# One more block product of a two-level Winograd product as seven 256x256 products (Q4, groups 2 to 4)

## The reference

```python
y   = einsum('bct,bcd->bdt', x, weights[condition])   # x: (64, 64, 1024), weights[condition]: (64, 64, 64)
xf  = y.reshape(4096, 1024)
G   = zeros(4096, 64); the 16 largest of xf @ Wr.T get softmax gates
h   = einsum('nd,krd->nkr', xf, A)                    # A: 64 x 16 x 1024, so h is 4096 x 1024
out = einsum('nkr,kdr->nd', h * G[:, :, None], B)     # again 1024 -> 1024
return x + 2.0 * out
```

## Time and profile before

| | us |
|---|---|
| median of 3 runs | 715.38 (714.88 to 715.78) |
| the profiled execution | 715.06 |
| its span | 713.3 |
| PE busy | 707.2 (99%) |
| DVE busy | 499.8 (70%) |
| ACT busy | 259.5 (36%) |
| DMA moved | 186.85 MB, 262 GB/s over the span |

### The profile page before, as it was taken

One profiled execution on the slowest core, in us unless ns is written; L12 is line 12 of the kernel. 1 busy time (PEld: TensorE's weight loads), 2 busy tenths in 40 slices (PEclk: granted clock), 3 DMA queues, 4 the chain that ended last, 5 costly groups with the idle time before them and its releaser, 6 DMA issues.

```text
span 713.3 us, 10128 instructions
## 1 busy us (share of the span) xinstructions
PE 707.2 (99%) x3522; PEld 599.8 (84%) x3522; DVE 499.8 (70%) x897; ACT 259.5 (36%) x475; POOL 1.6 (0%) x6
## 2 busy tenths in 40 slices
PE   9999999999999999999999999999999999999997
PEld 8888888888888888888898888888889888888886
DVE  5888999995558796745572868774557297777665
ACT  5675553525326431223332552132233353213210
POOL 0000000000000000000000000000000000000000
PEclk9999999999999999999999999999999999999999
DMA  9976679666798968467588775765758787536756
GB/s 323 405 299 279 219 278 397 221 245 228 272 371 329 335 239 296 154 231 242 201 305 344 282 280 165 263 202 193 284 204 317 304 307 256 194 129 201 253 209 221
DMA packets 59716, 186.85 MB, mean 262 GB/s; under 512 B 9874, under 2 KB 12562, under 8 KB 59154
## 3 DMA queue, kind: packets, MB, share of 16 engines
q1 hardware_dynamic: 57746, 182.68, 70.6%
q10 hardware_dynamic: 1920, 3.54, 1.4%
HBM read 136.38 MB, written 49.81 MB: 261 GB/s over the span
## 4 chain that ended last, share of the span: by engine, by line
PE 98%; DVE 1%; issue 1%; POOL 0%; DVEq 0%; POOLq 0%
PE Pb L572 42%; PE Pb L605 38%; PE Cb L554 8%; PE S L636 4%; PE Pb L625 4%; PE T L643 1%; PE T L690 0%; PE T L684 0%; PE Pb L588 0%; DVE Q L913 0%; PE Cb L650 0%; DVE Ox L913 0%; PE S L650 0%; PE T L650 0%; DVE Op L913 0%
## 5 line engine op out<-in xcount | busy, mean ns | idle before, releaser
L572 PE MATMUL Pb<-Op,Wt 128*128 128x512 f32 x984 | 237.6, 391 | 0.0
L605 PE MATMUL Pb<-Wt,Op 128*128 128x512 f32 x912 | 218.1, 391 | 0.0
L572 PEld LDWEIGHTS Pb<-Op,Wt 128*128 128x128 f32 x984 | 183.3, 188 | 37.5
L605 PEld LDWEIGHTS Pb<-Wt,Op 128*128 128x128 f32 x912 | 170.0, 188 | 34.9 <-DVE Op L913 0.4
L913 DVE TENSOR_TENSOR Q<-Pb,Q 128x1024 f32<-128x1024 f32 (+1 forms) x77 | 82.4, 1077 | 64.4 <-issue 54.3
L750 ACT COPY R<-Cb 128x512 f32<-128x512 f32 x60 | 35.1, 587 | 144.3 <-PE Cb L554 144.2
L913 DVE TENSOR_TENSOR Op<-R,Op 128x512 fp32r<-128x512 f32 x93 | 61.6, 684 | 22.7 <-ACT Op L724 22.7
L572 PE MATMUL Pb<-Ox,Wt 128*128 128x512 f32 x300 | 75.6, 390 | 0.0
L605 PE MATMUL Pb<-Wt,Ox 128*128 128x512 f32 x288 | 73.0, 391 | 0.0
L572 PEld LDWEIGHTS Pb<-Ox,Wt 128*128 128x128 f32 x300 | 56.1, 188 | 11.6
L913 DVE TENSOR_TENSOR Cq<-Pb,Cq 128x1024 f32<-128x1024 f32 (+1 forms) x40 | 40.2, 1006 | 32.2 <-issue 22.9
(11 more groups left out here) (94 smaller groups left out, 505.2 us busy)
## 6 DMA issues: line engine op xcount, KB each, us to landing
Wt<-Wd SPq DMA_DIRECT2D x177, 512.0 KB, 5.5
Wd<-Wt SPq DMA_DIRECT2D x56, 512.0 KB, 4.8
Q<-in_x SPq DMA_DIRECT2D x32, 512.0 KB, 5.6
xc<-in_x SPq DMA_DIRECT2D x24, 512.0 KB, 3.9
out<-Q SPq DMA_DIRECT2D x19, 512.0 KB, 4.0
out<-Q SPq DMA_DIRECT2D x26, 256.0 KB, 3.7
Wd<-xc SPq DMA_DIRECT2D x7, 512.0 KB, 6.3
BR<-in_B SPq DMA_DIRECT2D x3, 1024.0 KB, 8.1
```

The costliest lines, as they stand in the source:

```text
L572: t = e.matmul(Pb[:, j, :], Wt[:, k, a, 128 * c:128 * c + 128], part((USES1[m], s, c), z), start=fresh and (c, a, z) == (0, 0, 0), stop=(c ...
L605: t = e.matmul(Pb[:, i, :], part((USES2[m], s, c), a)[:, 128 * i:128 * i + 128], Wt[:, k, z, :], start=fresh and (c, a, z) == (0, 0, 0), s ...
```

## The change

Q4 (`m` = 4) joins Q3 as seven 256x256 products in groups 2 to 4 (`TWO`). Its operand G22 is split in seven forms, with four more sums on VectorE; the forms that are sums take Cq[:, 3] (Q4) and `u` (Q3) as their place. S4's sums move from Q7's steps to Q6's. Before the seven products Q7's accumulated banks are added to Q7's and to Q4's place. Of the four tiles that are added to the place of seven-product blocks, three are added ahead of these, the fourth behind the first of the seven.

The weights of Q4 need seven more forms. They are made in group 1's second stage, at the steps 20 to 26: ScalarE copies (`made_hi`, behind `unit_hi`, ahead of the step's operand splits), VectorE subtracts (`made_lo`, ahead of `unit_lo`) and makes four sums between, SyncE stores a form to `Wd` in the step after (`made_store`, behind `weights_load`, ahead of `unit_store` and `q_store`). They go through the two halves of one buffer, so that the copy of form n (n from 2) waits until the store of form n-2 has landed.

```diff
+TWO = [(), (4, 6), (4, 6), (4, 6)]
+LEVEL = (4, 6)
...
-MADE_AT = [0, 2, 4, 6, 12, 13, 15]
+MADE_AT = {4: [20, 21, 22, 23, 24, 25, 26], 6: [0, 2, 4, 6, 12, 13, 15]}
...
 def steps(s, m):
-    return 7 if s and m == 6 else 4
+    return 7 if m in TWO[s] else 4
...
+def cond_step(s, m, i):
+    step = 4 * m + i
+    if s + 1 == NS or i > 3:
+        return None
+    if s == 0:
+        return SPREAD.index(step) if step in SPREAD else None
+    return step // 3 if step in range(2, 24, 3) else None
...
 def splits_second(s, m, c):
+    if m == 3 and 4 in TWO[s]:
+        return [("G22", k) for k in ((0, 1), (2,), (3,), (4,))[c]]
+    if m == 4 and 4 in TWO[s]:
+        return [("G22", c + 5)] if c < 2 else [("S1", c - 2)] if c < 6 else []
...
# SyncE
+            def made_store(m, n):
+                e.wait_ge(v_made, made_before(m) + n + 1)
+                e.dma_start(Wd[UNITS + 7 * LEVEL.index(m) + MADE[n]], made(m, n)).then_inc(o_made[n % 2], 16)
...
                for m, name in enumerate(SECOND):
                    for i in range(steps(s, m)):
                        step = 4 * m + i
-                        weights_load(BASE[s] + 28 + 4 * m + (i if s and m == 6 else 0))
+                        weights_load(BASE[s] + USED[s].index(UNITS + 7 * LEVEL.index(m) + i if m in TWO[s] else 28 + 4 * m))
+                        if s == 0 and step - 1 in MADE_AT[4]:
+                            made_store(4, MADE_AT[4].index(step - 1))
                         if s == 0 and m < 6:
                             unit_store(32 + step)
...
# TensorE, two(s, m, k)
                 elif k == 3:
-                    e.wait_ge(v_out, out_done(s, 5, 3, 1))
+                    e.wait_ge(v_out, out_done(s, m - 1, 2, 1))
...
# ScalarE
+            def made_hi(m, n):
                 if n >= 2:
-                    e.wait_ge(o_form[n % 2], 16 * (n // 2))
+                    e.wait_ge(*stored(m, n - 2))
+                elif m == 6:
+                    e.wait_ge(p_cond, rows_number(1, 6 + n, 0))
                 else:
-                    e.wait_ge(p_cond, rows_number(1, 6 + n, 0))
+                    e.wait_ge(v_wlo, 52)
                 if n > 2:
-                    e.wait_ge(v_twow, n - 2)
-                e.copy(made(k, 0).bitcast(F32R), weight2(k)).then_inc(a_twohi, 1)
+                    e.wait_ge(v_wsum, 4 * LEVEL.index(m) + n - 2)
+                e.copy(made_part(m, n, 0).bitcast(F32R), weight2(m, MADE[n])).then_inc(a_made, 1)
...
                             unit_hi(32 + step)
+                        if s == 0 and step in MADE_AT[4]:
+                            made_hi(4, MADE_AT[4].index(step))
                         for name, c in splits_second(s, m, i):
...
# VectorE
+            def made_lo(m, n):
+                e.wait_ge(a_made, made_before(m) + n + 1)
+                add(made_part(m, n, 1).bitcast(F32R), weight2(m, MADE[n]), made_part(m, n, 0), v_made, ALU.subtract)
+                a11, a12, a21, a22 = weight2(m, 0), weight2(m, 1), weight2(m, 4), weight2(m, 6)
                 if n == 1:
+                    if m == 6:
+                        e.wait_ge(v_wlo, UNITS)
+                    add(a21, a11, a21, v_wsum, ALU.subtract)
                 elif n == 2:
...
+                    add(a22, a22, a21, v_wsum, ALU.subtract)
...
+                    add(a11, a22, a11, v_wsum)
+                elif n == 3:
+                    add(a12, a12, a22, v_wsum, ALU.subtract)
...
# VectorE, drain_second
                 add(to, P, to, v_out, n=2)
-                if s and name == "Q5":
-                    to = Q[:, 3 + i:5 + i, 512:1024]
-                    e.wait_ge(v_out, out_done(s, 2, i))
-                    add(to, P, to, v_out, n=2)
+                if m + 1 in TWO[s]:
+                    tile, half = INTO[SECOND[m + 1]][0] + i, INTO[SECOND[m + 1]][1]
...
+                    if i == 1:
+                        to = Q[:, tile - 1:tile + 1, 512 * half:512 * half + 512]
+                        add(to, P, to, v_out, n=2)
+                    else:
+                        to = Q[:, tile - 1, 512 * half:512 * half + 512]
+                        add(to, Pb[:, 2, :], to, v_out)
...
# VectorE, drain_two
+                add(to, Pb[:, BANK2[r], :].rearrange("p (i n) -> p i n", n=256), to, v_out)
+                if r == 0:
+                    tile, half = INTO[SECOND[m]]
+                    to = Q[:, tile + 3, 512 * half:512 * half + 512]
+                    add(to, Pb[:, 3, :], to, v_out)
...
# VectorE, the second stage
+                        if s == 0 and step in MADE_AT[4]:
+                            made_lo(4, MADE_AT[4].index(step))
                         if s == 0 and m < 6:
                             unit_lo(32 + step)
```

More of the change, by code:

```diff
@@ L22 @@
 SENT = -3.4028234663852886e38
+TWO = [(), (4, 6), (4, 6), (4, 6)]
+LEVEL = (4, 6)
+USED = [[*range(28)] + [n for m in range(7) for n in (
+    range(56 + 7 * LEVEL.index(m), 63 + 7 * LEVEL.index(m)) if m in TWO[s] else range(28 + 4 * m, 32 + 4 * m))]
+    for s in range(NS)]
+BASE = [sum(len(u) for u in USED[:s]) for s in range(NS + 1)]
 FIRST = ["P2", "P1", "P5", "P3", "P6", "P7", "P4"]
@@ L143, in chunk_done, with chunk_done2, form_done, level_before @@
     return 49 * s + 7 * m + 4 + c
+def chunk_done2(s, m, c):
+    return 7 * sum(k not in TWO[r] for r in range(s + 1) for k in range(7 if r < s else m)) + 4 + c
 def tile_done2(s, m, i):
[L148 to L157, removed]
-def split_done(name, s, c):
-    return 4 * s + c + 1 if name != "S4" or s == 0 else 7 * s - 3 + c + 1
+    return chunk_done2(s, m, 0) - 4 + (i + 1 if i < 3 else 7)
+def form_done(s, m, k):
+    return 7 * level_before(s, m) + k + 1
+def level_before(s, m):
+    return sum(len(TWO[r]) for r in range(s)) + TWO[s].index(m)
+def split_done(name, s, c):
+    m = USES2.index(name) if name in USES2 else 0
+    return sum(steps(r, m) for r in range(s)) + c + 1
+def outs():
+    order = []
+    for s in range(NS):
+        for m in range(7):
+            if m in TWO[s]:
+                order += [(s, m, 0, 0), (s, m - 1, 3, 1), *((s, m, i, 0) for i in range(1, 7))]
+            elif m + 1 in TWO[s]:
+                order += [(s, m, i, r) for i, r in ((0, 0), (1, 0), (0, 1), (1, 1), (2, 0), (3, 0), (2, 1))]
+            else:
+                order += [(s, m, i, 0) for i in range(4)]
+    return {key: n + 1 for n, key in enumerate(order)}
+OUTS = outs()
 def out_done(s, m, i, r=0):
[L168 to L171, removed]
+    return OUTS[s, m, i, r]
 def unit_use(n):
     s = max(s for s in range(NS) if BASE[s] <= n)
[L177 to L183, removed]
+    return s, USED[s][n - BASE[s]]
 def rows_number(s, i, a):
@@ L315, in quarter, with weight2, made, made_before @@
             return block[:, 2 * c:2 * c + 2, 256 * n:256 * n + 256]
-        def weight2(k):
+        def weight2(m, k):
             c, n = [(0, 0), (1, 0), (1, 1), (0, 0), (0, 1), (1, 0), (1, 1)][k]
[L320 to L329, removed]
+            return (u if m == 4 else raws[2])[:, 2 * c:2 * c + 2, 256 * n:256 * n + 256]
+        def made(m, n):
+            return raws[1][:, 2 * (n % 2):2 * (n % 2) + 2, :].rearrange("p a n -> p (a n)") if m == 4 else xc[:, n % 2, :]
+        def made_before(m):
+            return 7 * LEVEL.index(m)
+        def stored(m, n):
+            return o_made[n % 2], 16 * (n // 2 + 1) + (64, 48)[n % 2] * LEVEL.index(m)
+        def made_part(m, n, a):
+            return made(m, n)[:, 512 * a:512 * a + 512].rearrange("p (c n) -> p c n", n=256)
+        def out2(m, r):
+            (tile, half), (t, n) = INTO[SECOND[m]], INTO2[r]
+            at = 512 * half + 256 * t
+            return Q[:, tile + 2 * n:tile + 2 * n + 2, at:at + 256]
+        def places2(m):
+            return (Cq[:, 1, :, :], Cq[:, 3, :, :]) if m == 4 else (Cq[:, 2, :, :], u[:, :, :])
         def source(name, s, c):
@@ L444, in x_load @@
                     if s == 2:
-                        e.wait_ge(o_form[i], (64, 48)[i])
+                        e.wait_ge(*stored(6, 6 - i))
                 else:
@@ L486, in _ @@
                         weights_load(BASE[s] + step)
[L487 to L490, removed]
+                        if s == 1 and step - 1 in MADE_AT[6]:
+                            made_store(6, MADE_AT[6].index(step - 1))
                         if s == 0 and 6 <= step < 10:
@@ L700, in _ @@
                         step = 4 * m + i
-                        if s and m == 6:
-                            two(s, i)
+                        if m in TWO[s]:
+                            two(s, m, i)
                         else:
                             second(s, m, i)
-                        if more and step in (SPREAD if s == 0 else range(2, 24, 3)):
-                            k = SPREAD.index(step) if s == 0 else step // 3
+                        k = cond_step(s, m, i)
+                        if k is not None:
                             e.wait_ge(l_w[k], 32 * (s + 1))
@@ L935, in made_lo @@
```

(1 more changed line is left out.)

185 lines of the change are left out of this document (98 added, 87 removed).

## The result

The changed kernel takes 736.47 us (median of 4 runs, 736.13 to 737.77) against 715.45 before: 1.0298 times as long, 95% interval 1.0280 to 1.0316. The profiled execution took 736.34 us, its span is 734.6, so the span grew by 21.3 us. The prediction said 734, range 728 to 741.

A forecast was written before the change was run, and what follows sets the result against it. TensorE, busy 99%, was taken to bound the kernel. From 715.06 us, less 1.8 gained, plus 18.5 for waits and 2.1 for the clock, came 733.9; with 0.3 for the median 734.2, said as 734, range 728 to 741.

The forecast's parts named there:

- The ring: End of group 1: drain, store, landing, copy, subtraction, drain in series, three times round; TensorE 18.5 us late.
- store 0: First form's store in group 1, behind an output store: issued at 182.15, landed after 5.5 us at 187.65.
- S4's fourth part: Split read by tile 24 of group 1: ready at 193.9, wanted at 188.14, so 5.9 us late.
- Store 3: Form store near the end of group 1: issued at 200.75, 5.64 us after the drain's end at 195.1.
- Store 3's landing: Queued behind four weight loads: 7.0 us, landing at 207.75, with copy 5 and y21 part two behind it.
- store 4's: Landing with the queue nearly empty: 3.8 us, at 215.1, ahead of copy 6 and y21 parts three and four.
- the stores are hidden: Rival for group 1: stores issued when forms are ready cost nothing; 713.6 us, 0.4 us of slack; 5% faster, 2% no change.
- The clock: TensorE's restart after standing still for 6 and 7 us: 2.1 us lost once, between 0 and 4.2.
- The gain: Seven narrow products for Q4 in groups 2 to 4: 0.83 + 0.83 + 0.15 = 1.8 us gained.
- What is late next is that load: Group 4's last block: the sixth product waits for its last two weights' load, so adding the fourth tile later gains 0.

The follow-up runs named there:

- outputs_later: Changed kernel, with the eight output stores of Q5 and Q3 in group 1 issued behind the group's last step: 721.32 us, 1.0087 of the kernel before.
- pool_queue: Changed kernel, with the stores of Q4's seven weight forms issued from GpSimd's queue instead of SyncE's: 722.86 us, 1.0111 of the kernel before.
- pair_drain: Changed kernel, but Q4's forms made in group 2, Q3's last two form loads earlier, fourth tile added with the third before the seven products: 720.03 us, 1.0065.
- shift: Kernel before, with only S4's sums moved to Q6's steps and the fourth tile added behind the first product, no forms of Q4: 715.35 us, 1.0002.
- shift_early: As shift, with the loads of Q3's last two weight forms issued ahead of the output store: 714.47 us, 0.9988 of the kernel before.
- before_early: Kernel before, with only the loads of Q3's last two weight forms issued early: 715.02 us, 0.9995 of the kernel before.
- spread: Changed kernel, with fourteen forms of Q3 and Q4 spread over group 2's first stage and Q3's last two form loads early: 714.42 us, 0.9986.

## Why the prediction was right

The mechanism, its place and its size came out.

**The ring.** Predicted 18.5 us, measured 20.4. Its members are the chain above. By steps: store 0 predicted at 182.15, issued at 182.45, landed after 5.65 us (5.5). S4's fourth part predicted ready at 193.9, TensorE went on at 194.98. Store 3 predicted at 200.75, issued at 202.54: I had let store 1's landing (6.31 us, from 185.44) hide behind ScalarE's other copies, and it ended 1 us later than they did; the rest is SyncE's list, which took 6.5 us from the drain's end to store 3 instead of 5.64. Store 3's landing took 8.3 us against 7.0, store 4's 3.0 against 3.8. These are the mis-sized terms: 1.8 + 1.3 - 0.8, less the 0.34 us by which the whole kernel starts later, 1.9 us in all. That the last of the three erred the other way is luck; it brought the sum 0.8 us nearer. One wait was left out: group 2's first tile also waits for the drain of its bank, 7.6 us (213.99); it ends ahead of the wait for y21's third part, so it costs nothing. outputs_later and pool_queue show the lock of stores and drains to be worth 13 to 15 us. In outputs_later a wait of 5.0 us for landings in series through two buffers is left, with 1.8 us for the clock behind it.

My rival "the stores are hidden" (5%) was worked out with every store issued as its form is ready: store 3 near 186 and landed by 193. No run met that condition. In outputs_later store 3 was issued at 190.50, 3.9 us after its form was ready, and in pool_queue at 190.63, 4.3 us after; the times were 721 and 723, not 713.6. The rival's working also took 7.2 us at most for a landing, where 9.1 and 9.4 were measured behind the four loads. With its slack of 0.4 us either alone could undo it; whether it would hold with stores issued at once stays open.

**The clock.** Predicted one loss of 2.1 us, measured 1.91 at group 2's first tiles. The size came out, but the place is another than I had in mind. In the standstill of 7.6 us the granted clock fell from 1.00 to 0.50, the lower level of 1.2 GHz. TensorE had stopped at 206.4 and the clock was 1.00 until 210; at the end of the kernel before it had fallen within 2 us of the last matmul. It was 0.50 from 214 to 216, for most of the six matmuls; what that costs is hidden, since TensorE waits 2.4 us behind them for y21's third part. At 218 the clock was back at 1.00. It fell once more, to 0.50 between 221 and 223, while TensorE worked, behind that wait; this second dip makes the 18 matmuls 1.91 us longer. The Trainium skill (TensorE: Matmul & The Clock Gate, "What's actually happening") states that the half rate is the default and that activity releases it; the trace agrees for the fall in the standstill and the rise behind the six matmuls. The second dip began while TensorE was busy, behind a wait of 2.4 us, and that sentence alone does not tell it. I had not expected the loss in the first gap either: after waits of 4.1 and 1.9 us the clock was 0.64 on average between 195 and 202, and 39 matmuls took 11.45 us; at 0.227 us each, with the 0.2 us by which such a row is longer, they would take 9.0. These 2.4 us are hidden, since TensorE waits for y21 behind them anyway.

**The gain.** Predicted 1.8 us, measured 1.36. Q4 gives 0.8 in groups 2 and 3 as worked out: 48 wide matmuls, 10.90, became 2.87 + 7.18 = 10.05. Q3's seven products then take 10.16 instead of 10.07 with the shift (pair_drain shows it in both groups), and in group 4 the sixth product waits 0.94 instead of 0.29 us for its weights. In group 4 Q4 takes 10.81 us (697.37 to 708.18), against 10.75 by the working. The 0.227 us of the rows held, the 0.120 became 0.121 with the shift. By the distance that the Trainium skill states (TensorE: Matmul & The Clock Gate, "Wait — 56ns, not 53.3ns?") the estimate was 3.6 us for three groups; the trace does not agree (0.227 us from one matmul of 512 columns to the next, not 0.216).

**The last load.** "What is late next is that load": shift, shift_early and before_early bear it out in their traces; in time only shift_early's interval leaves the kernel before out.

What was not tried: more than two buffers for the forms in group 1, which is what the waits for landings in outputs_later would need.

## What to carry to other kernels

A store that frees a buffer is a link of the compute path: look at what stands ahead of it in the issuing queue, and what the wait on its landing stands ahead of on the engine that waits. Work that is free by the busy shares (ScalarE 36%) can cost more than ten times the gain (22.7 us against 1.4) through waits in one order. Give such a store the distance of its slowest landing (9.7 us in the earlier trace rows), not of its median (6.3); spread does so with mostly four steps of 2.72 us.

## What the runs showed of the hardware

- The landings of the forms' stores (512 KB, to HBM, from SyncE's queue) that are named above took between 3.0 and 9.4 us, and longer where more was queued ahead: 3.0 behind one output store of 256 KB, 5.7 and 6.3 among other stores, 8.3 to 9.4 behind four loads of 512 KB.
- TensorE stood still for 4.1 us, worked for 0.96, and stood still for 1.9; in the 7 us that followed the granted clock was 0.64 on average.
- The granted clock fell to 0.50 between 221 and 223 while TensorE was busy throughout; it had waited 2.4 us before 219.33.
- GpSimd's queue issued a store of 512 KB only when the one before had landed (issues at 183.03, 190.63, 198.50, with the data ready 4.3 and 6.8 us earlier for the last two). SyncE's queue held several at once: in the kernel before four loads were issued within 3.45 us and landed 7.0 us after their issue.
- SyncE needed 5.2 us to issue eight loads of 16 KB (0.64 each) and 3.4 us for four of 512 KB (0.86 each): a burst of small transfers delays the issue of what stands behind it about as much as large ones do.
